# A graph layer on one core: a ring of 24 gathered chunks instead of 84, and all degree rows kept in SBUF

## The chip, the core and the metric

One core of one Trainium2 chip runs the whole kernel. The metric is the device time of one launch in microseconds (us); lower is better. TensorE is called PE here, VectorE DVE, ScalarE ACT, GpSimd POOL and SyncE SP, as the profile does.

## The reference, cut to what matters

There are 50,000 nodes with 128 features each, and 100,000 edges sorted by their target node (each node has at least the edge to itself). For each node the source rows of its edges are summed, and then:

```
h_self  = x @ W_self.T + b_self
messages = x[src] @ W_neigh.T + b_neigh
h_neigh = segment_sum(messages, dst)          # sum over the edges of each target node
out = layernorm(x + relu(h_self + h_neigh))   # over the 128 features
```

The kernel moves the product behind the sum: it sums gathered rows of x per target node and multiplies the sums by W_neigh once. The bias b_neigh then has to be added as often as the node has edges, its degree.

## The kernel before, in words

**The work.** The 50,000 nodes are 391 tiles of 128, taken in 131 groups of three, called trios (`tau` in the code). The self edges are left out of the gather (they go into `wsum` = W_self + W_neigh), so 50,000 edges remain, packed into 391 chunks of 128 edges, three to a trio.

**Preparation (the first 55 us or so).** DVE finds, with help of PE and POOL, where each of the chunks and tiles begins in the edge list. Lists are then made in three parts: chunks 0 to 98 (trios 0 to 32) before the loop, chunks 99 to 197 and 198 to 390 inside the loop by `later_lists(t)` on DVE and PE; the second part is there after loop step 11, the third after step 39. The same code finds the degree of each node (`degrees_start`, `degrees_bits`, `degrees_end`), in three parts too: tiles 0 to 98 before the loop, tiles 99 to 197 by step 19, and the rest by step 55.

**The gather.** POOL issues one indirect DMA for each chunk (line 467): 128 rows of x, 64 KB in all, into slot `c % RING` of the tile `ring`. Before the first chunk of a trio it waits until the trio eight earlier has landed (eight semaphores, `gathered`), and before every chunk from `RING` on until enough trios were summed: `triples_summed >= (c - RING) // 3 + 2`.

**The loop, for each trio.** PE sums gathered rows per target node (`sum_chunks`: two passes for `carry`, line 887, and six matmuls with one-hot tiles `pick`, line 893) and then raises `triples_summed`; DVE builds `pick` beforehand (line 728). ACT copies the sums to `sums_t` (line 994). PE turns the trio's rows of x (line 877), and ACT copies them to `x_t` (line 1002). Then `products` on PE: one bf16 matmul adds the biases, with a tile `degrees_t` of 12 rows as weights (line 908: nine rows hold the degrees of three tiles, three times each since the bias is split in three bf16 parts, and three rows hold 1.0), and twelve fp32 passes follow, six of x at line 912 and six of the sums at line 913; the last raises `h_done`. DVE adds x after the relu (line 739, `y_done`) and takes statistics, ACT normalises (line 1021), and SP stores the result (line 380). PE sums two or three trios ahead of the one whose products it makes. All orders are written out by hand; each engine works through its own list, and semaphores join them.

**SP's queue.** For each trio: load x of that trio (after `y_done` of four trios earlier), load its degree rows from the DRAM scratch `degrees_dram` into one of four tiles `degrees_t` (after `h_done` of four trios earlier), and store the result of the trio six earlier. At loop steps 33 and 66, and once before the loop, `store_degrees` first writes a part of the degrees from SBUF to `degrees_dram` and waits for it to land.

Of the kernel before, what the change touches and what calls it, by code (L numbers as in the profile page):

```python
# [19 lines left out]
BF16 = mybir.dt.bfloat16  # L20
# [5 lines left out]
P = 128  # L26
NODES, DIM, EDGES = 50000, 128, 100000
# [15 lines left out]
COLUMNS = 4  # L43
SPREAD = 99
# [9 lines left out]
TRIO = 3  # L54
TRIOS = -(-TILES // TRIO)
FIRST_TRIOS = SPREAD // TRIO
DEEP = 4
PARTS = 3
BIAS_ROWS = (TRIO + 1) * PARTS
# [14 lines left out]
TIGHT_LOW = 14  # L74
TIGHT_HIGH = 117

RING = 84
GATHER_SEMS = 8
SUM_BANKS = 3
LOAD = 4  # L80
# [91 lines left out]
def build_common_case(nc, ctx, k, x, src, dst, out):  # L172
    def sb(name, shape, dtype=FP32):
        return ctx.enter_context(nc.sbuf_tensor(name, shape, dtype))

    def sem(name):
        return ctx.enter_context(nc.semaphore(name))
# [69 lines left out]
    pick = [sb(f"pick{i}", [P, PICK]) for i in range(DEEP)]  # L247
    sums_t = sb("sums_t", [P, LAP + MARGIN])
    x_t = [sb(f"x_t{i}", [P, TRIO, P]) for i in range(2)]
    degrees_t = [sb(f"degrees_t{i}", [BIAS_ROWS, P], BF16) for i in range(DEEP)]  # L250
    y = [sb(f"y{i}", [P, TRIO, DIM]) for i in range(DEEP)]
    stats = [sb(f"stats{i}", [P, TRIO, 6]) for i in range(DEEP)]
    mean_var = [sb(f"mean_var{i}", [P, TRIO, 2]) for i in range(DEEP)]
# [27 lines left out]
    offsets_known = sem("offsets_known")  # L281
    locals_known = sem("locals_known")
    degrees_done = sem("degrees_done")
    degrees_stored = sem("degrees_stored")
    dve_order = sem("dve_order")
    checks_done = sem("checks_done")
# [2 lines left out]
    gathered = [sem(f"gathered{i}") for i in range(GATHER_SEMS)]  # L289
    sums_cleared = sem("sums_cleared")  # L290
    x_landed = [sem(f"x_landed{i}") for i in range(DEEP)]
    degrees_landed = [sem(f"degrees_landed{i}") for i in range(DEEP)]
    pick_built = sem("pick_built")
    triples_summed = sem("triples_summed")
    sums_placed = sem("sums_placed")
# [4 lines left out]
    h_done = sem("h_done")  # L300
# [9 lines left out]
    def tiles_of(tau):  # L310

        return (1, LAST_ROWS) if tau == TRIOS - 1 else (TRIO, P)
# [17 lines left out]
    with nc.Block() as block_:  # L330

        @block_.sync
        def _(sp):
            sp.dma_start(end_dst[:], dst.rearrange("(b e) -> b e", e=BLOCK)[:, BLOCK - 1:BLOCK].rearrange("b o -> o b"),
                         allow_slow_non_contiguous=True).then_inc(ends_landed, 16)
            for padded, edges in ((dst_padded, dst), (src_padded, src)):
                sp.dma_start(padded[0:EDGES, :].rearrange("(p e) o -> p (e o)", p=EDGE_ROWS),
                             edges.rearrange("(p e) -> p e", p=EDGE_ROWS)).then_inc(padded_stored, 16)
            sp.wait_ge(pads_set, 2)
            for a, padded in enumerate((src_padded, dst_padded)):  # L340
                sp.dma_start(padded[EDGES:EDGES + PAD, :].rearrange("e o -> o e"), pads[:, a, :]).then_inc(padded_stored, 16)
            sp.dma_start(k.ws[:], w_self).then_inc(k.weights_landed, 16)
            sp.dma_start(k.wn[:], w_neigh).then_inc(k.weights_landed, 16)
            sp.dma_start(k.bs_row[:], b_self.rearrange("(a d) -> a d", a=1)).then_inc(k.weights_landed, 16)
            sp.dma_start(k.bn_row[:], b_neigh.rearrange("(a d) -> a d", a=1)).then_inc(k.weights_landed, 16)
            sp.dma_start(k.bn[:], b_neigh.rearrange("(a d) -> a d", a=1).partition_broadcast(P)).then_inc(k.bn_landed, 16)

            def load_x(tau):
                if tau >= DEEP:
                    sp.wait_ge(y_done, tau - DEEP + 1)  # L350
                sp.dma_start(x_in[tau % DEEP][0:tiles_of(tau)[1], 0:tiles_of(tau)[0], :], rows_of(x, tau)).then_inc(x_landed[tau % DEEP], 16)

            def load_degrees(tau):
                tiles, _ = tiles_of(tau)
                if tau >= DEEP:
                    sp.wait_ge(h_done, tau - DEEP + 1)
                sp.dma_start(degrees_t[tau % DEEP][0:tiles * PARTS, :],
                             degrees_dram[tau * TRIO * PARTS:(tau * TRIO + tiles) * PARTS, :]).then_inc(degrees_landed[tau % DEEP], 16)

            def store_degrees(part, j0, j1):  # L360

                sp.wait_ge(degrees_done, part)
                for j in range(j0, j1):
                    sp.dma_start(degrees_dram[j * SPREAD * PARTS:(j + 1) * SPREAD * PARTS, :].rearrange("(p a) n -> p a n", a=PARTS),
                                 degrees[:, j, :].unsqueeze(1).to_broadcast([SPREAD, PARTS, P])).then_inc(degrees_stored, 16)
                sp.wait_ge(degrees_stored, 16 * j1)

            def load_edges():

                sp.dma_start(edge_src[:], src.rearrange("(p e) -> p e", p=EDGE_ROWS)).then_inc(edges_landed, 16)  # L370
                sp.dma_start(edge_dst[:, 0:EDGE_COLS], dst.rearrange("(p e) -> p e", p=EDGE_ROWS)).then_inc(edges_landed, 16)
                sp.wait_ge(next_set, 1)
                sp.dma_start(edge_dst[0:EDGE_ROWS - 1, EDGE_COLS:EDGE_COLS + 1],
                             dst.rearrange("(p e) -> p e", p=EDGE_ROWS)[1:EDGE_ROWS, 0:1],
                             allow_slow_non_contiguous=True).then_inc(next_landed, 16)

            def store(tau):
                tiles, rows = tiles_of(tau)
                sp.wait_ge(result_done, tau + 1)
                sp.dma_start(rows_of(out, tau), result[tau % DEEP][0:rows, 0:tiles, :]).then_inc(stored[tau % DEEP], 16)  # L380

            sp.wait_ge(k.parts_made, 3)
            sp.wait_ge(window_landed[0], 32)
            for q in range(TRIO):
                sp.dma_start(k.bias[q * PARTS:(q + 1) * PARTS, q, :], k.bias_part[:, :, 0, :]).then_inc(k.parts_landed, 16)
                sp.dma_start(k.bias[TRIO * PARTS:BIAS_ROWS, q, :], k.bias_part[:, :, 1, :]).then_inc(k.parts_landed, 16)

            for tau in range(DEEP):
                load_x(tau)
            store_degrees(1, 0, 1)  # L390
            for tau in range(DEEP):
                load_degrees(tau)
            for tau in range(DEEP, TRIOS + DEEP + 2):
                if tau == FIRST_TRIOS:
                    store_degrees(2, 1, 2)
                if tau == FIRST_TRIOS + DEEP:
                    load_edges()
                if tau == 2 * FIRST_TRIOS:
                    store_degrees(3, 2, COLUMNS)
                if tau < TRIOS:  # L400
                    load_x(tau)
                    load_degrees(tau)
                if tau >= DEEP + 2:
                    store(tau - DEEP - 2)
            for i in range(DEEP):
                sp.wait_ge(stored[i], 16 * len(range(i, TRIOS, DEEP)))
# [76 lines left out]
        def _(dve):  # L483
# [6 lines left out]
                dve.wait_ge(dve_order, chain[0])  # L490

            v = nc.vector
            v.memset(pads[:, 0, :], 0).then_inc(pads_set, 1)
            v.memset(pads[:, 1, :], NODES).then_inc(pads_set, 1)
            v.memset(edge_dst[:, EDGE_COLS:EDGE_COLS + 1], NO_NODE).then_inc(next_set, 1)
# [10 lines left out]
            v.memset(k.ones[:], 1.0)  # L506
            v.memset(k.eps[:], EPS)
            v.memset(checks[:], 0.0)
            for i in range(DEEP):
                v.memset(degrees_t[i][:], 1.0)  # L510
            link(v.memset(k.bias[:], 0.0))

            def find_blocks(a, j0, j1):
# [271 lines left out]
            def later_lists(t):  # L785
# [12 lines left out]
                    degrees_bits(1, 2, [t - 11])  # L798
                if t == 13:
                    spread_lists(2, FIRST_TRIOS, 2 * FIRST_TRIOS, FIRST_TRIOS - 1, 2 * FIRST_TRIOS - 1)  # L800
                if t == 19:
                    degrees_end(1, 2)
                if t == 20:
# [14 lines left out]
                    shift_move(2, COLUMNS, (t - 39) // 2)  # L818
                if t == 41:
                    spread_lists(3, 2 * FIRST_TRIOS, ENTRIES // TRIO, 2 * FIRST_TRIOS - 1, TRIOS - 1)  # L820
                if t == 55:
                    degrees_end(2, COLUMNS)
                if t == 60:
# [36 lines left out]
        def _(pe):  # L860
# [36 lines left out]
            def products(tau):  # L897

                b = tau % 2
                tiles, rows = tiles_of(tau)  # L900
                pe.wait_ge(degrees_landed[tau % DEEP], 16 * (tau // DEEP + 1))
                pe.wait_ge(xt_copied, tau + 1)
                if tau >= 2:
                    pe.wait_ge(y_done, tau - 1)
                pe.wait_ge(sums_placed, sums_needed(tau))
                if tau in joined_at:
                    pe.wait_ge(laps_joined, joined_at[tau])
                mm(h_bank[b][0:rows, 0:tiles * DIM], degrees_t[tau % DEEP][:, 0:rows], k.bias[:, 0:tiles, :], start=True, stop=False)  # L908
                for q in range(tiles):
                    h = h_bank[b][0:rows, q * DIM:q * DIM + DIM]  # L910
                    at = (tau * TRIO + q) * P % LAP
                    mm(h, x_t[b][:, q, 0:rows], k.wsum_t[:], start=False, stop=False)  # L912
                    ins = mm(h, sums_t[:, at:at + rows], k.wn_t[:], start=False, stop=(q == tiles - 1))  # L913
                ins.then_inc(h_done, 1)
# [360 lines left out]
```

## Time and profile before

| | us |
|---|---|
| three runs | 804.57, 804.39, 798.32 (median 804.39) |
| the profiled execution, its own time | 803.84 |
| its span, first to last instruction | 802.0 |
| PE busy | 557.8 (70%) |
| DVE busy | 446.4 (56%) |
| POOL busy | 403.5 (50%) |
| ACT busy | 303.2 (38%) |

The rows below come from that one execution. The 1.84 us between its span and its own time lie around the instructions. The granted TensorE clock was 0.865 of full speed on average. Of the DMA engines' time 23.7% went to the queue of SP's transfers and 12.9% to POOL's gathers.

### The profile page before, as it was taken

The page shows a single profiled execution, that of the slowest core. Times are in us where ns is not written, and L with a number is a line of the kernel's source. Part 1 is how long each engine was busy: PE and PEld are TensorE (multiplying, and loading weights), DVE is VectorE, ACT ScalarE, POOL GpSimd, SP SyncE. Part 2 cuts the span into 40 slices and gives each one's busy share as a digit, 9 for nine tenths or more (in the row PEclk, how much of TensorE's full clock was granted, in tenths as well). Part 3 has the DMA queues.
Part 4 walks back from the last instruction along what each step waited for, and adds up shares of the span by engine and source line. Part 5 has one row for each costly group of instructions (what it writes and reads, how often), then busy time and mean ns, then how long its engine had stood idle before and what let it go on. Part 6 is the DMA issues. An engine that isn't in the chain of part 4 may idle for free. (4 is left out here: it accounts for less than half of the span.)

```text
span 802.0 us, 11397 instructions
## 1 busy us (share of the span) xinstructions
PE 557.8 (70%) x3151; PEld 441.7 (55%) x3151; DVE 446.4 (56%) x1927; ACT 303.2 (38%) x789; POOL 403.5 (50%) x424
## 2 busy tenths in 40 slices
PE   2054011069742979888678886978897988999995
PEld 0033001048631767666557675756675776778784
DVE  8880100048812777776566757565554555566765
ACT  0000000025311535444234544535453544566566
POOL 5777777520375656660756666556565666100000
PEclk9998555559955989998879999889997999999998
DMA  2421211123312434453334443444444444433433
GB/s 76 120 56 52 62 52 52 43 60 101 104 52 63 127 113 128 132 150 95 102 93 134 123 133 110 123 114 132 115 136 112 131 123 134 119 105 101 116 104 93
DMA packets 122933, 82.12 MB, mean 102 GB/s; under 512 B 15374, under 2 KB 115894, under 8 KB 122840
## 3 DMA queue, kind: packets, MB, share of 16 engines
q1 hardware_dynamic: 109208, 53.63, 23.7%
q0 software_dynamic: 13664, 27.77, 12.9%
q8 instruction: 26, 0.43, 0.2%
q14 instruction: 35, 0.29, 0.1%
HBM read 55.44 MB, written 26.71 MB: 102 GB/s over the span
## 5 line engine op out<-in xcount | busy, mean ns | idle before, releaser
L467 POOL DMA_INDIRECT ring<-in_x,chunk_src x391 | 378.7, 968 | 271.7 <-issue 110.9
L994 ACT COPY sums_t<-bank 128x496 f32 x131 | 74.8, 571 | 423.9 <-remote 202.2
L893 PE MATMUL bank<-pick,ring 128*128 128x192 f32 (+2 forms) x782 | 231.9, 437 | 4.0 <-DMA ring<-in_x,chunk_src 4.0
L739 DVE SCALAR_TENSOR_TENSOR y<-bank,x_in 128x384 f32<-128x384 f32 x131 | 72.6, 554 | 215.7 <-remote 173.2
L912 PE MATMUL bank<-wsum_t,x_t 128*128 128x128 f32 (+1 forms) x782 | 175.4, 307 | 15.2 <-issue 15.2
L913 PE MATMUL bank<-wn_t,sums_t 128*128 128x128 f32 (+1 forms) x782 | 160.8, 287 | 24.2 <-issue 24.2
L1021 ACT ACTIVATE result<-y,minus_mean,rstd 128x128 f32<-128x128 f32 x391 | 163.4, 486 | 0.0
L893 PEld LDWEIGHTS bank<-pick,ring 128*128 128x128 f32 x782 | 146.1, 210 | 19.0 <-issue 4.3
L912 PEld LDWEIGHTS bank<-wsum_t,x_t 128*128 128x128 f32 (+1 forms) x782 | 126.6, 203 | 40.0 <-issue 39.8
L913 PEld LDWEIGHTS bank<-wn_t,sums_t 128*128 128x128 f32 (+1 forms) x782 | 127.6, 204 | 24.8 <-issue 24.8
L887 PE MATMUL bank<-carry,ring 128*128 128x1 f32 x260 | 44.6, 241 | 106.8 <-DVE pick L728 77.8
L728 DVE TENSOR_SCALAR pick<-columns,local 128x192 f32<-128x192 f32 (+2 forms) x391 | 117.9, 357 | 0.2
L887 PEld LDWEIGHTS bank<-carry,ring 128*128 128x128 f32 x260 | 42.6, 206 | 120.6 <-DVE pick L728 87.5
L759 DVE BATCH_NORM_STATS2 stats<-y 128x6 f32<-128x128 f32 x391 | 87.4, 277 | 0.2
L1002 ACT COPY x_t<-bank 128x384 f32<-128x384 f32 x131 | 63.1, 482 | 54.9 <-remote 24.9
L775 DVE RECIPROCAL rstd<-std 128x3 f32<-128x3 f32 x131 | 21.9, 168 | 105.4 <-ACT std L1011 89.4
L877 PEld LDWEIGHTS bank<-identity,x_in 128*128 128x128 f32 x391 | 54.9, 151 | 41.7 <-issue 12.8
L877 PE MATMUL bank<-identity,x_in 128*128 128x128 f32 x391 | 69.5, 289 | 9.3 <-issue 5.6
L908 PE MATMUL bank<-bias,degrees_t 12*128 12x384 bf16 x131 | 45.6, 348 | 43.2 <-issue 37.1
L908 PEld LDWEIGHTS bank<-bias,degrees_t 12*128 12x128 bf16 x131 | 12.0, 91 | 69.1 <-issue 65.6
L1011 ACT ACTIVATE std<-mean_var,eps 128x3 f32<-128x3 f32 x131 | 40.2, 307 | 0.4 <-DVE mean_var L767 0.4
L767 DVE BATCH_NORM_AGGREGATE mean_var<-stats 128x2 f32<-128x6 f32 x391 | 38.6, 154 | 0.0
(122 smaller groups left out, 207.9 us busy)
## 6 DMA issues: line engine op xcount, KB each, us to landing
x_in<-in_x SPq DMA_DIRECT2D x130, 192.0 KB
out<-result SPq DMA_DIRECT2D x130, 192.0 KB
ring<-in_x,chunk_src POOLq DMA_INDIRECT x391
degrees_t<-degrees_dram SPq DMA_DIRECT2D x130, 2.2 KB
dst_padded<-in_dst SPq DMA_DIRECT2D x1, 390.6 KB
src_padded<-in_src SPq DMA_DIRECT2D x1, 390.6 KB
edge_src<-in_src SPq DMA_DIRECT2D x1, 390.6 KB
edge_dst<-in_dst SPq DMA_DIRECT2D x1, 390.6 KB
```

The source lines that it names most:

```text
L467: nc.gpsimd.indirect_dma_start(ring[:, c % RING, :], None, x, bass.IndirectOffsetOnAxis(ap=chunk_src[:, c:c + 1], axis=0)).then_inc(gather ...
L728: ins = v.tensor_scalar(pick[tau % DEEP][:, PICK_AT[q]:PICK_AT[q] + hi - lo], columns[:, lo:hi], local[:, c:c + 1], None, ALU.is_equal)
L739: v.scalar_tensor_tensor(y[tau % DEEP][0:rows, 0:tiles, :], h_bank[b][0:rows, 0:tiles * DIM].rearrange("p (q d) -> p q d", q=tiles), 0.0, ...
L759: ins = v.bn_stats(stats[b][0:rows, q, :], y[b][0:rows, q, :])
L877: ins = nc.tensor.transpose(xt_bank[b][:, q * P:q * P + rows], x_in[tau % DEEP][0:rows, q, :], k.identity[0:rows, 0:rows])
L887: mm(sums[:, 0:1], ring[:, (tau * TRIO - 1) % RING, :], carry[:, tau - 1:tau], start=True, stop=False, skip_group_check=True)
L893: ins = mm(sums[:, lo:hi], ring[:, c % RING, :], pick[tau % DEEP][:, PICK_AT[q]:PICK_AT[q] + hi - lo], start=(tau == 0 and q == 0), stop=( ...
L912: mm(h, x_t[b][:, q, 0:rows], k.wsum_t[:], start=False, stop=False)
L913: ins = mm(h, sums_t[:, at:at + rows], k.wn_t[:], start=False, stop=(q == tiles - 1))
L994: nc.scalar.copy(sums_t[:, bass.ds(at, SPAN)], sum_bank[tau % SUM_BANKS][:, 0:SPAN]).then_inc(sums_placed, 1)
L1002: nc.scalar.copy(x_t[b][:, 0:tiles, 0:rows], xt_bank[b][:, 0:tiles * P].rearrange("p (q w) -> p q w", q=tiles)[:, :, 0:rows]).then_inc(xt_ ...
L1021: ins = nc.scalar.activation(result[b][0:rows, q, :], y[b][0:rows, q, :], ACT.Identity, bias=minus_mean[b][0:rows, q:q + 1], scale=rstd[b] ...
```

## The change

Two things are changed at once. `RING` goes from 84 to 24. And the four tiles `degrees_t` with one transfer for each trio become one tile with a place for every trio (12 rows, 132 places of 128 bf16 values), filled by four transfers: `store_degrees` issues them itself, one for each of the four groups of 33 trios, behind its wait for the write to DRAM. DVE sets each quarter of the tile to 1.0 beforehand, the first before the loop and the others at steps 12, 40 and 42; SP waits for that (`degrees_set`). PE waits for `degrees_landed` only at trios 0, 33, 66 and 99.

```diff
-RING = 84
+RING = 24
...
-    degrees_t = [sb(f"degrees_t{i}", [BIAS_ROWS, P], BF16) for i in range(DEEP)]
+    degrees_t = sb("degrees_t", [BIAS_ROWS, TRIOS + 1, P], BF16)
...
-            def load_degrees(tau):
-                tiles, _ = tiles_of(tau)
-                if tau >= DEEP:
-                    sp.wait_ge(h_done, tau - DEEP + 1)
-                sp.dma_start(degrees_t[tau % DEEP][0:tiles * PARTS, :],
-                             degrees_dram[tau * TRIO * PARTS:(tau * TRIO + tiles) * PARTS, :]).then_inc(degrees_landed[tau % DEEP], 16)
-
             def store_degrees(part, j0, j1):
 
                 sp.wait_ge(degrees_done, part)
+                sp.wait_ge(degrees_set, j1)
                 for j in range(j0, j1):
                     sp.dma_start(degrees_dram[j * SPREAD * PARTS:(j + 1) * SPREAD * PARTS, :].rearrange("(p a) n -> p a n", a=PARTS),
                                  degrees[:, j, :].unsqueeze(1).to_broadcast([SPREAD, PARTS, P])).then_inc(degrees_stored, 16)
                 sp.wait_ge(degrees_stored, 16 * j1)
+                for j in range(j0, j1):
+                    first = j * FIRST_TRIOS
+                    sp.dma_start(degrees_t[0:TRIO * PARTS, first:first + FIRST_TRIOS, :],
+                                 degrees_dram[j * SPREAD * PARTS:(j + 1) * SPREAD * PARTS, :].rearrange("(t r) n -> r t n", r=TRIO * PARTS)
+                                 ).then_inc(degrees_landed, 16)
...
-            for tau in range(DEEP):
-                load_degrees(tau)
...
-                    load_degrees(tau)
...
+            def set_degrees(j):
+
+                v.memset(degrees_t[:, j * FIRST_TRIOS:(j + 1) * FIRST_TRIOS, :], 1.0).then_inc(degrees_set, 1)
+
...
-            for i in range(DEEP):
-                v.memset(degrees_t[i][:], 1.0)
+            set_degrees(0)
             link(v.memset(k.bias[:], 0.0))
...
+                if t == 12:
+                    set_degrees(1)
...
+                if t in (40, 42):
+                    set_degrees(t // 2 - 18)
...
-                pe.wait_ge(degrees_landed[tau % DEEP], 16 * (tau // DEEP + 1))
+                if tau % FIRST_TRIOS == 0:
+                    pe.wait_ge(degrees_landed, 16 * ((1, 2, COLUMNS, COLUMNS)[tau // FIRST_TRIOS]))
...
-                mm(h_bank[b][0:rows, 0:tiles * DIM], degrees_t[tau % DEEP][:, 0:rows], k.bias[:, 0:tiles, :], start=True, stop=False)
+                mm(h_bank[b][0:rows, 0:tiles * DIM], degrees_t[:, tau, 0:rows], k.bias[:, 0:tiles, :], start=True, stop=False)
```

## Rows read from the trace of the kernel before

**Rows 1.** The page: busy tenths in 40 slices of 20 us.
```profile
PE   2054011069742979888678886978897988999995
...
POOL 5777777520375656660756666556565666100000
```

**Rows 2.** Waits, whole span: engine, line, releaser, us in total, times, longest.
```profile
ACT sums_t L994 <- remote: 202.2, 31, 56.3
...
DVE y L739 <- remote: 173.2, 22, 61.9
...
POOL ring L467 <- DVE chunk_dst L668: 52.8, 3, 32.4
```

**Rows 3.** Timeline of PE, 60 to 170 us: start, us, what.
```profile
63.20 2.90 PE L893 MATMUL bank<-pick,ring 128*128 128x192 f32 x6
...
76.50 0.37 PE L913 MATMUL bank<-wn_t,sums_t 128*128 128x128 f32 x1 [1.03 <-issue]
99.20 0.59 PE L887 MATMUL bank<-carry,ring 128*128 128x1 f32 x2 [22.33 <-issue]
...
165.21 0.59 PE L887 MATMUL bank<-carry,ring 128*128 128x1 f32 x2 [21.15 <-DVE pick L728]
```

**Rows 4.** Timeline of DVE and of ACT, the same stretch.
```profile
97.58 0.56 DVE L739 SCALAR_TENSOR_TENSOR y<-bank,x_in 128x384 f32<-128x384 f32 x1 [39.43 <-remote]
...
119.99 0.57 ACT L994 COPY sums_t<-bank 128x496 f32 x1 [56.30 <-remote]
```

**Rows 5.** Windows: stretch, its us, busy of PE, PEld, DVE, ACT, POOL (with counts), PEclk, DMA share, GB/s.
```profile
66.10:170.50 104.40, 15.83 (x51) 10.77 (x49) 6.08 (x21) 1.80 (x4) 67.66 (x72) 0.55 0.17 49
177.70:210.00 32.30, 31.62 (x194) 25.53 (x193) 28.17 (x124) 18.42 (x48) 0.00 (x1) 0.93 0.33 95
415.00:682.80 267.80, 227.92 (x1348) 181.74 (x1346) 161.72 (x738) 127.03 (x334) 162.55 (x168) 0.94 0.46 125
```

**Rows 6.** Timeline of POOL: the gather behind each pause.
```profile
170.52 0.94 POOL L467 DMA_INDIRECT ring<-in_x,chunk_src  x1 [15.13 <-PE bank L893]
...
257.42 1.05 POOL L467 DMA_INDIRECT ring<-in_x,chunk_src  x1 [6.37 <-remote]
...
407.89 1.04 POOL L467 DMA_INDIRECT ring<-in_x,chunk_src  x1 [4.18 <-remote]
...
470.05 0.94 POOL L467 DMA_INDIRECT ring<-in_x,chunk_src  x1 [0.30 <-issue]
473.13 1.05 POOL L467 DMA_INDIRECT ring<-in_x,chunk_src  x1 [2.14 <-remote]
```

**Rows 7.** Waits of POOL between 415 and 682.8 us.
```profile
POOL ring L467 <- remote: 31.8, 15, 2.8
POOL ring L467 <- PE bank L893: 25.7, 12, 5.5
```

**Rows 8.** Timeline of PE at the end: the sums of the last two trios.
```profile
784.56 1.59 PE L893 MATMUL bank<-pick,ring 128*128 128x192 f32 x6
...
788.26 0.57 PE L893 MATMUL bank<-pick,ring 128*128 128x192 f32 x2
```

**Rows 9.** Groups of instructions, shapes apart: DVE's memsets.
```profile
L747 DVE MEMSET sums_t<- 128x512 f32 x12 | 5.8, 485 | 2.1 <-DVE sums_t L746 1.7 <-issue 0.3
...
L510 DVE MEMSET degrees_t<- 12x128 bf16 x4 | 0.6, 165 | 0.0
```

**Rows 10.** Timeline of DVE, SP and PE around the first degrees.
```profile
8.02 0.74 DVE L515 TENSOR_SCALAR_CACHE_REDUCE below<-bank,limit 99x500 f32<-99x500 f32 x1 [1.08 <-PE bank L864]
...
55.63 0.89 SPq L364 DMA_DIRECT2D degrees_dram<-degrees  x1
58.30 1.41 SPq L357 DMA_DIRECT2D degrees_t<-degrees_dram  x4
...
59.76 0.50 PE L908 MATMUL bank<-bias,degrees_t 12*128 12x384 bf16 x1 [2.78 <-DMA degrees_t<-degrees_dram]
```

**Rows 11.** Waits of SP's DMA queue, whole span.
```profile
SPq L380 <- ACT result L1021: 198.1, 92, 5.3
```

More of the change, by code:

```diff
@@ L283, in build_common_case @@
     degrees_done = sem("degrees_done")
+    degrees_set = sem("degrees_set")
     degrees_stored = sem("degrees_stored")
@@ L291, in build_common_case @@
     x_landed = [sem(f"x_landed{i}") for i in range(DEEP)]
-    degrees_landed = [sem(f"degrees_landed{i}") for i in range(DEEP)]
+    degrees_landed = sem("degrees_landed")
     pick_built = sem("pick_built")
```

## The prediction

> **What bounds the kernel now.** I began with the slices of the page, since a mean hides that this kernel has stretches with different limits [rows 1]. Between 80 and 160 us (fifth to eighth slice) PE is nearly idle while POOL is at 5 to 7 tenths. From 700 us on POOL does nothing and PE stands at 9 tenths. In between both are busy. The waits over the whole span come next [rows 2]: ACT waited 202.2 us ahead of its copy of the sums, DVE 173.2 us ahead of y, with single waits of 56.3 and 61.9 us. For both no releaser is named, though the work they wait for is PE's.
>
> The timelines show what such a wait is. The sums of trio 3 end at 63.20 + 2.90 = 66.1 us [rows 3], but ACT's copy, which waits for them, starts at 119.99 [rows 4]. The first `h_done` is raised by the pass just ahead of 63.20, and DVE's y starts at 97.58. PE has idle gaps of 22.33 and 21.15 us and trickles between them. So PE's finished work is seen by the others 34 to 54 us late. Meanwhile POOL issues one gather after another: 72 in 104.4 us, beside 51 matmuls of PE, while the DMA engines are busy for 0.17 of the time only [rows 5]. This is no lack of bandwidth. In the stretch from 177.7 to 210.0 there is no gather: PE makes 194 matmuls in 32.3 us and is busy for 31.6 of them. That is 6.0 matmuls a microsecond against 0.5.
>
> What ends such a stretch is POOL's own pause [rows 6]: the gather at 170.52 stands behind 15.13 us of idleness, those at 257.42 and 407.89, which end shorter runs of gathers, behind 6.37 and 4.18, and in the steady part the pauses are about 2.14. I read it so: while POOL gathers without a pause, PE's signals are delivered far too slowly, and a pause lets them through. Longer runs need longer pauses. The rows don't show which resource is shared; the argument needs only the pattern.
>
> The steady part, 415 to 682.8 us, then has a simple account. A gather takes 0.94 us and 0.30 to the next [rows 6], 1.25 in all. 168 gathers, 56 trios, fill 168 x 1.25 = 210 us, and the waits of POOL are 31.8 + 25.7 = 57.5 us in 27 pauses of 2.13 [rows 7]: together 267.5 of 267.8. The cadence is 267.8 / 56 = 4.78 us a trio. Without gathers it is 788.26 - 784.56 = 3.70 [rows 8]. The bound is thus this alternation for most trios, PE for the last 26 or so, and for over 100 us at the start neither: the signals are stuck.
>
> **The ring.** With 84 slots POOL may run 26 trios ahead, so at the start it has no reason to pause. With 24 slots chunk c >= 24 waits for `triples_summed` >= (c - 24) // 3 + 2, about six trios ahead. Step by step:
> - Gathers begin at about 38.4 us. Chunks up to 29 need at most three summed trios, known long before. Chunk 30 needs the fourth, whose signal at 66.1 is late. POOL therefore stops after 30 gathers, at 38.4 + 30 x 1.25 = 75.9 us instead of about 155.
> - The signals then get through. The pauses behind shorter and longer runs were 4.18, 6.37 and 15.13 us [rows 6]; 30 gathers are nearest to the run of 33 that ended at 251 us, so I take 6 us. Then DVE makes y and the picks of trio 4, and PE sums trio 4 at about 83.7 us instead of 99.65. From below the pause costs 2.14, from above 15.13.
> - From then on POOL is held by its credits throughout, as it was between 415 and 682.8. I take that cadence, 4.78 us, for trios 4 to 124. Three other things vanish: the stretch up to 170 us, the wait for the list of chunks (52.8 us in all [rows 2]) with the burst behind it, and, on the debit side, the fast trios at 3.70 us, since gathers now accompany nearly all of them. Lists are ready in time: chunk 99 is asked for when trio 26 is summed, and its list is made at step 11.
> - Gathers end about six trios ahead of PE: 6 x 3.70 = 22.2 us, then from the last sum to the end 802.0 - 788.3 = 13.7, as now.
> A ring of six to seven trios can't starve PE at this cadence: it holds some 29 us of work, and a gather needs its own 1.25 us and its landing.
>
> **The degrees.** Four memsets of 128 values (165 ns each) become one of 33 x 128 = 4224. Between 128 and 512 values a memset grows from 165 to 485 ns [rows 9], 0.83 ns a value, so 4224 cost 165 + 4096 x 0.83 = 3.6 us. Behind the old ones DVE idled 1.08 us for PE before 8.02 us [rows 10]; the start becomes later by 3.6 - 0.6 - 1.1 = 1.9 us (none if the fill runs several values at a time, 2.9 if the idle time can't be used). The three inside the loop, 3.6 us each, stand on DVE ahead of the next y and picks; with DVE busy 161.72 of 267.8 us [rows 5], 0.4 of each lies in slack. I count 1 us each, 3 in all, between 0 and 11.
>
> At the start the tile's transfer follows the write to DRAM. Now the write is issued at 55.63, the loads at 58.30, and PE goes on at 59.76. One load of all 297 pieces is as large as the write, which needed 2.67 us: 1.2 us later for PE, at most 4 if it takes twice as long. This hardly shows in POOL's pause, which is set by the gathers.
>
> What is removed: 131 issues on SP at 1.41 / 4 = 0.35 us each. SP waited 198.1 us for ACT's results alone [rows 11], so this lies in idle time, and I take nothing for it. PE has one wait less for each trio; where gathers hold up its signals that might bring a little, where they don't its matmuls are the limit. I take 0, and as the other bound 0.05 us x 131 = 6.6 us. At trios 33, 66 and 99 PE needs a load that SP issued three or more trios earlier, over 10 us: hidden. If that cover were gone, it would cost about 3 us each.
>
> **The sum.** Trio 4 summed from 83.7 + 1.9 = 85.6. 120 trios x 4.78 = 573.6: 659.2. Six trios and the tail, 35.9: 695.1. Memsets 3: 698. Around the span lie 803.84 - 802.0 = 1.8: 700 us. The profiled execution is within 0.6 us of the median 804.39, so I compare with that directly: 0.87 of it.
>
> **The rivals.**
> - *Small steps with a pause for each (slower).* In the steady part POOL made 168 / 27 = 6.2 gathers between pauses. The handshake could settle at three, each with the pause of 2.13 us: 3.75 + 2.13 = 5.88 us a trio, and the sum is 85.6 + 706 + 35.9 + 3 + 1.8 = 832. It decides from a cadence of 5.65. For it: a short ring gives credits one trio at a time. Against: the old ring did so too once it was full.
> - *POOL becomes the only bound (faster).* If evenly spread gathers leave PE's signals alone, the cadence is POOL's own 3.75: 85.6 + 450 + 35.9 + 3 + 1.8 = 576. For it: the 3.70 without gathers. Against: the steady part, where POOL was held back likewise and lost 1.03 us for each trio.
> - *The first stretch stays.* If the stuck signals are released by something other than POOL's pause, PE reaches trio 6 at 176 us as now, and 118 trios at 4.78 follow: 176 + 564 + 35.9 + 3 + 1.8 = 781.
> - *The gathers are innocent.* [Rows 5] show 0.5 matmuls a microsecond beside gathers and 6.0 without. Then both would have a third cause, the ring would change nothing, and only the memsets would be left: 804 + 1.9 + 3, near 808. The Trainium skill's page "SBUF — State Buffer", section "Who interferes with whom", speaks for this rival: only the port pair that VectorE and GpSimd share causes contention, and a DMA never contends with a compute engine, so gathers could not hold up TensorE. The rows here disagree with a reading of that rule that extends it to signals: PE stands still beside gathers while DVE is idle too.
>
> **How the numbers follow.** Forecast 0.78, small steps 0.06, POOL the bound 0.07, the first stretch stays 0.05, gathers innocent 0.04. Within the forecast the cadence matters most: with a pause only after nine gathers it is 3.75 + 2.13 / 3 = 4.46, 38 us less; after 4.5 gathers it is 5.17, 47 us more. The start adds 9 us and the memsets and the first load up to 11 upwards, the start 4 and PE's lighter list 7 downwards; not all at once. The range is 655 to 745. A difference under 1% can't be told from none. Faster by over 1%: 0.78 + 0.07 + 0.05 = 0.90; same 0.04; slower 0.06.
>
> **What the changed profile would show.** Slices of PE from the fifth on at 6 tenths or more; POOL busy to near the end in every slice at about 6 to 7 tenths, with no wait for `chunk_dst`; gathers 415 to 682.8 still about 168; no single wait of ACT or DVE over 15 us; POOL's first long pause near 76 to 78 us; three memsets near 3.6 us in the loop, and four issues of `degrees_t`. I am wrong if the cadence beside gathers differs from 4.78, if POOL's first pause is as long as 15 us, or if PE waits for `ring`.

## The result and the profile after

The changed kernel took 707.26 us (median of 4 runs, 706.41 to 711.72), the kernel before beside it 804.48 (4 runs, 798.32 to 807.9): a ratio of 0.881, with a 95% interval of 0.8745 to 0.8875. The profiled execution took 706.77 us with a span of 705.0; its granted clock averaged 0.928 against 0.865. The prediction said 700 in a range of 655 to 745.

One thing has to be said beside this number. In the runs of this study the unchanged kernel before showed two times: about 800 us in four sets of runs (this one among them) and about 582 us in two others. All that follows about a gain holds where the kernel before takes 800 us. Where it took 582, neither the ring of 24 nor the wait alone changed the time, and the changed kernel as it is was not run.

The slices of the page after, to be read against [rows 1]: 40 slices, now of 17.6 us.
```profile
PE   2036388988797878697987879788898978979995
...
POOL 3777565666666656555655646565555666555600
```
The hole of four slices in PE is one slice deep (the fifth, at 3), and POOL gathers to near the end. Waits over the whole span, to be read against [rows 2]: engine, line, releaser, us in total, times, longest. "Remote" stands where the view names no releaser.
```profile
ACT sums_t L1000 <- remote: 192.5, 43, 24.4
...
POOL ring L464 <- remote: 85.2, 39, 4.8
...
DVE y L740 <- remote: 78.1, 28, 10.4
...
POOL ring L464 <- PE bank L898: 54.8, 30, 5.8
```
The longest wait of ACT fell from 56.3 to 24.4 us and that of DVE from 61.9 to 10.4; POOL's waits are now many and short. The wait of POOL for `chunk_dst` is gone. Now the start. The timelines of PE, of SP's queue (the first load of the degrees) and of POOL between 61 and 90 us, to be read against [rows 3] and [rows 6]:
```profile
64.36 0.49 PE L914 MATMUL bank<-bias,degrees_t 12*128 12x384 bf16 x1 [4.45 <-DMA degrees_t<-degrees_dram]
...
72.76 1.59 PE L898 MATMUL bank<-pick,ring 128*128 128x192 f32 x6
...
85.86 0.50 PE L914 MATMUL bank<-bias,degrees_t 12*128 12x384 bf16 x1 [7.74 <-ACT x_t L1008]
...
89.29 2.35 PE L898 MATMUL bank<-pick,ring 128*128 128x192 f32 x6
```
```profile
61.26 0.32 SPq L364 DMA_DIRECT2D degrees_t<-degrees_dram  x1
```
```profile
79.75 0.94 POOL L464 DMA_INDIRECT ring<-in_x,chunk_src  x1 [0.30 <-issue]
85.51 0.94 POOL L464 DMA_INDIRECT ring<-in_x,chunk_src  x1 [4.81 <-remote]
```
POOL stopped at 79.75 + 0.94 = 80.7 us and waited 4.81 us. PE stands still for the 7.74 us before 85.86, 2.6 of them before POOL's stop, and goes on 0.35 us after POOL does. The trio summed at 72.76 is trio 4, before POOL's stop; trio 5 follows 16.5 us later.

Windows of after: stretch, its us, busy of PE, PEld, DVE, ACT, POOL (with counts), PEclk, DMA share, GB/s, to be read against [rows 5].
```profile
80.00:160.00 80.00, 63.18 (x361) 50.60 (x361) 58.39 (x228) 33.97 (x86) 47.50 (x49) 0.89 0.40 108
89.30:415.00 325.70, 273.11 (x1565) 215.89 (x1565) 245.42 (x969) 148.08 (x387) 197.28 (x198) 0.92 0.46 123
100.00:640.00 540.00, 457.26 (x2647) 361.89 (x2648) 356.39 (x1522) 252.84 (x662) 326.81 (x334) 0.93 0.46 124
415.00:640.00 225.00, 192.34 (x1130) 152.59 (x1130) 117.04 (x573) 108.35 (x286) 136.25 (x142) 0.94 0.46 124
```
Between 80 and 160 us PE now makes 361 matmuls, 4.5 a microsecond, where it made 51 in the 104.4 us of [rows 5]. From 100 to 640 us POOL makes 334 gathers, 111.3 trios: 4.85 us a trio. The steady stretch of before had 4.78. So the whole kernel now runs at about the rate that its steady part had. Of the 97.0 us between the two spans, 76.4 are gained up to the sums of trio 5, which start at 89.3 instead of 165.7, and 20.7 between trio 5 and trio 124 (579.7 us instead of 600.4): less time lost up to 415 us, fewer fast trios at the end. The sums of trio 124 start at 669.0, 36.0 us ahead of the end, as before (35.9).

### The profile page after: what moved, and what is told of

Same layout as the page of the kernel before. It is cut to its first block and busy times, and to the rows that moved or that the text cites. A ratio compares the mean times of both kernels' runs of the same rounds, so it can differ in the third digit from the quotient of the medians.

```text
span 705.0 us, 11177 instructions
## 1 busy us (share of the span) xinstructions
PE 551.2 (78%) x3151; PEld 434.3 (62%) x3151; DVE 461.1 (65%) x1927; ACT 303.2 (43%) x789; POOL 410.1 (58%) x424
## 5 line engine op out<-in xcount | busy, mean ns | idle before, releaser
L464 POOL DMA_INDIRECT ring<-in_x,chunk_src x391 | 385.2, 985 | 244.9 <-issue 104.4
L918 PE MATMUL bank<-wsum_t,x_t 128*128 128x128 f32 (+1 forms) x782 | 170.9, 302 | 1.9 <-issue 1.9
L919 PE MATMUL bank<-wn_t,sums_t 128*128 128x128 f32 (+1 forms) x782 | 156.5, 282 | 2.0 <-issue 1.8
L898 PEld LDWEIGHTS bank<-pick,ring 128*128 128x128 f32 x782 | 144.4, 208 | 20.7 <-issue 5.2
L918 PEld LDWEIGHTS bank<-wsum_t,x_t 128*128 128x128 f32 (+1 forms) x782 | 123.4, 198 | 27.6 <-issue 27.5
L919 PEld LDWEIGHTS bank<-wn_t,sums_t 128*128 128x128 f32 (+1 forms) x782 | 124.1, 200 | 1.5 <-issue 1.5
L729 DVE TENSOR_SCALAR pick<-columns,local 128x192 f32<-128x192 f32 (+2 forms) x391 | 119.8, 361 | 0.2
L892 PEld LDWEIGHTS bank<-carry,ring 128*128 128x128 f32 x260 | 41.2, 199 | 87.2 <-DVE pick L729 78.5
L882 PE MATMUL bank<-identity,x_in 128*128 128x128 f32 x391 | 71.1, 294 | 7.4 <-DMA x_in<-in_x 4.4
```

The source lines that it names most:

```text
L464: nc.gpsimd.indirect_dma_start(ring[:, c % RING, :], None, x, bass.IndirectOffsetOnAxis(ap=chunk_src[:, c:c + 1], axis=0)).then_inc(gather ...
L729: ins = v.tensor_scalar(pick[tau % DEEP][:, PICK_AT[q]:PICK_AT[q] + hi - lo], columns[:, lo:hi], local[:, c:c + 1], None, ALU.is_equal)
L882: ins = nc.tensor.transpose(xt_bank[b][:, q * P:q * P + rows], x_in[tau % DEEP][0:rows, q, :], k.identity[0:rows, 0:rows])
L892: mm(sums[:, 0:1], ring[:, (tau * TRIO - 1) % RING, :], carry[:, tau - 1:tau], start=True, stop=False, skip_group_check=True)
L898: ins = mm(sums[:, lo:hi], ring[:, c % RING, :], pick[tau % DEEP][:, PICK_AT[q]:PICK_AT[q] + hi - lo], start=(tau == 0 and q == 0), stop=( ...
```

## The experiments

Three explanations stood at first. A: POOL's wait for summed trios, which comes after 24 chunks and makes it pause, is the whole gain. B: fewer slots matter by themselves (where the gathers land). C: the degree part brings something, by shorter lists on SP and PE or by its issues.

**The ring alone, and the wait alone.** The first is the kernel before with `RING` at 24. The second keeps 84 slots and changes the wait only:
```
+AHEAD = 24
...
-                if c >= RING:
-                    pool.wait_ge(triples_summed, (c - RING) // TRIO + 2)
+                if c >= AHEAD:
+                    pool.wait_ge(triples_summed, (c - AHEAD) // TRIO + 2)
```


> The kernel before with RING = 24 and nothing else. Theory A (POOL's unpaused gathers hold up PE's signals; the ring acts through POOL's earlier wait): nearly the whole gain is here, and a little more, since the 3.6 us memset at the start, the three in the loop and the longer first load of degrees are absent: 700 us, between 690 and 712. Rival C (the 131 small transfers were the burden, on SP's queue or on PE's waits): little is gained, 780 to 805.

> The kernel before with its tile of 84 slots, but POOL waits for triples_summed as with 24 slots. Theory A: the same as with RING = 24 alone, within 5 us, first pause of POOL after 30 gathers. Rival B (the size of the tile, the spread of the writes in SBUF or the reuse of slots matters): near 804.

Measured: 581.97 us (ratio 1.0002, 0.9974 to 1.0030) and 582.13 us (0.9994, 0.9976 to 1.0011), and the kernel before itself took 582.43 us in this set (19 runs, 578.58 to 583.96). No theory had this, and the set can't decide between A, B and C, since there was nothing to gain. The profile of the ring alone shows what is different. A window of the same stretch as the first of [rows 5], and the slices of the page:
```profile
66.10:170.50 104.40, 101.24 (x648) 83.06 (x647) 98.05 (x402) 60.40 (x155) 79.61 (x82) 1.00 0.54 148
```
```profile
PE   2017899999999889999997989999999999999994
...
POOL 4777777777777777777777767777777777777300
```
POOL made 82 gathers in this stretch, more than the 72 of [rows 5], and PE was busy for 101.24 of 104.4 us. POOL issued 231 gathers in one run, from 38.2 to 337.0 us, and where ACT waited for the sums, its copy began at most 0.9 us behind them. So a long run of gathers is not enough to hold up PE's signals: a condition outside the kernel must be present too. With it absent the cadence is 3.98 us a trio, near the 3.70 of [rows 8], and ring and wait are worth nothing.

The two levels differ only where gathers run. Up to the first gather there is no difference (38.4 us in before, 38.2 here), and the last six trios, from the sums of trio 124 to those of trio 130, take 22.2 us in both (766.06 to 788.26 and 543.69 to 565.89). So the 800 us are not those of a chip on which everything is slower.

**A shorter ring yet.** After with `RING = 12`, same set.

> The changed kernel with RING = 12. Theory A: two trios are summed early, so POOL pauses after 18 gathers, before PE's signals are stuck; the start gains some 10 us, and the cadence stays near 4.9 us a trio: 697 us. The rival of a too short ring: POOL may gather for a trio only when the one three earlier is summed, PE waits for ring, and the cadence grows to 5.9 us or more: 800 us or more.

Measured: 601.14 us, 1.0317 of before (1.0280 to 1.0353). Here too there was no lag to undo. POOL's waits with a named releaser end with PE's sums:
```profile
POOL ring L464 <- PE bank L898: 43.2, 29, 6.3
```
The cadence is 4.09 us against 3.98. It says nothing on the stuck signals. That a lead of two trios is on the short side is likely, but not shown alone: how much of the 19 us is the degree part's wasn't measured at this level.

**Gathers spaced out.** After, with a memset of 128x256 behind each gather. POOL works through its list in order, so the next gather stands behind the memset; each memset also waits for the one before it:
```
+                if c:
+                    pool.wait_ge(spaced_out, c)
+                nc.gpsimd.memset(spacer[:], 0.0).then_inc(spaced_out, 1)
```


> The changed kernel with a POOL memset of 128x256 behind each gather, which spaces the gathers from 1.25 to about 1.6 us. If what counts is how much POOL sends per unit of time (each gather needs a little more of a shared path than the 1.25 us in which it is issued), then PE's signals are no longer late and POOL's pauses vanish: 4.8 us a trio from three gathers at 1.6, the total about as the changed kernel, 690 to 710. If only POOL's full stops let signals through, the memsets add to the cadence: 3 x 0.35 = 1.05 us for each trio, 125 us in all, 830.

Measured in the first set: 640.78 us, 1.1001 of before (1.0963 to 1.1038). With 1.47 us from gather to gather POOL needs 4.41 us a trio and becomes the bound: the cadence was 4.40, and in the repeat below PE waited 35.7 us for the ring.

**Both kernels again.** The next set looked whether the 582 us would come back.

> The changed kernel once more, beside the kernel before on the same chip. Two readings of the first four experiments, in which the kernel before took 582 us and not 804: theory D, the late signals belong to the chip (or to its surroundings at the time) and not to the kernel; then on a chip without them this is the kernel before plus the memsets and the longer first load, 582 + 1 to 8 us, and on a chip with them 707 against 804. Rival E: something of the ring and degree parts together differs from the parts alone; then the ratio of 0.88 comes back even where the kernel before takes 582 us.

> The kernel before, for its profile. On a chip without late signals POOL gathers 84 and more chunks in one run, and yet ACT's copy of the sums starts 0.1 us behind them, PE is at 9 tenths from about 60 us on. On a chip with them the profile is that of 802 us again, with waits of 56 and 62 us near the start.

The 582 us did not come back: before had a median of 800.33 (7 runs), after 707.06 (700.6 to 710.17), ratio 0.882 (0.8751 to 0.8890), which repeats the first result. Rival E is therefore not tested here; the wait alone answers it further below. The profile of before again has a run of 93 gathers from 38.3 to 155.9 us, single waits of 57.0 (ACT) and 62.2 us (DVE), and PE at zero in the fifth and the eighth slice:
```profile
PE   2054021049733988889498887988888888999995
```

**Four kernels for the cause of the lag.** The next set was to tell whether POOL's issuing, the number of pieces or the bytes hold up the signals. `sp_loads` is before with 24 slots and no gathers at all: SP loads the 192 KB of each trio from neighbouring rows, so that other rows are summed. `narrow` is before with gathers of 128 B an index, and the other three quarters of each slot left at zero:
```
-                nc.gpsimd.indirect_dma_start(ring[:, c % RING, :], None, x,
+                nc.gpsimd.indirect_dma_start(ring[:, c % RING, 0:DIM // 4], None, x.rearrange("n (a d) -> (n a) d", a=4),
```


> Again the kernel before with 84 slots, POOL waiting as with 24, in the hope of a chip with late signals. If the kernel before takes about 800 here: theory A gives 700 (690 to 712), with the first pause of POOL after 30 gathers; rival B (size of the tile, reuse of slots) 800; rival C (the degree transfers) 785 to 800. If it takes about 582, this one does too.

> The changed kernel with a POOL memset of 128x256 behind each gather; gathers 1.47 us apart, and 640 us on a chip without late signals. On a chip with them: if a gather keeps a shared path busy for a little more than the 1.25 us in which POOL issues it, the spacing lets the signals through without pauses, the lags shrink to a microsecond or two, and the time comes down from 707 towards 640 to 660. If only POOL's full stops let signals through, the cadence is 4.4 + 1.1 us or more and the time 750 to 790.

> The kernel before with RING = 24 and no gathers: SP loads the ring, 192 KB for each trio in one plain transfer of neighbouring rows of x, so the sums are of other rows than the reference's. The same bytes land in the same tile. If the bytes or their landing hold up PE's signals, the cadence on a chip with late signals stays near 4.8 us a trio and the time near 700. If it is POOL's issuing, the lags are gone: PE at 3.70 us a trio, 575 to 590, and the same on any chip.

> The kernel before (84 slots) with gathers of 128 bytes for each index instead of 512, from x seen as rows of 32 values; three quarters of each slot stay at zero and the sums are not the reference's. The number of pieces, of gathers and of completions is unchanged. If the bytes matter, the first stretch loosens and the time falls to between 580 and 650; if the issuing or the pieces matter, it stays at 800 with PE idle between 80 and 160 us (on a chip without late signals it says nothing: 582).

Before took 582.2 us in this set (13 runs), and again nothing lagged: the wait alone 582.36 us (1.0012, 0.9987 to 1.0038), spaced 642.33 (one run), SP's loads 576.01 (one run), narrow 585.58 (one run, with its zeroing of the ring on POOL at the start). So these can't tell the causes apart. One thing they do suggest: with no gather at all the kernel took 576.01 us in its one run, 6 less than the median of before, so where signals are delivered at once the gathers cost about 1%.

**The wait alone where before takes 800 us.** The same kernel as the wait alone, once more.

> The kernel before with 84 slots and POOL waiting as with 24, a third time. Where the kernel before takes about 800: theory A gives 700 (690 to 712), POOL's first pause after 30 gathers, and with it the whole gain without the degree part and without fewer slots; rivals B and C give 785 to 800. Where the kernel before takes about 582, this one does too and the question stays open.

Now before had 801.47 us (6 runs), and the wait alone took 701.40 (4 runs, 693.47 to 705.64): ratio 0.8706, 0.8616 to 0.8795. The whole gain is there with all 84 slots and with the degrees as they were. B and C fall, A stands, and E with its ring and degree parts together is not needed. Its timeline of POOL at the first stop, and its window:
```profile
75.57 0.94 POOL L468 DMA_INDIRECT ring<-in_x,chunk_src  x1 [0.30 <-issue]
82.33 0.94 POOL L468 DMA_INDIRECT ring<-in_x,chunk_src  x1 [5.82 <-remote]
```
```profile
100.00:640.00 540.00, 457.46 (x2689) 364.03 (x2690) 350.97 (x1533) 256.52 (x672) 326.02 (x336) 0.94 0.46 126
```
It stops at 76.5 us for 5.82 us, as the prediction had it (75.9 and 6), and makes 336 gathers in the 540 us in which after made 334.

**Spaced where before takes 800 us.** The same kernel as in "Gathers spaced out".

> The changed kernel with a POOL memset of 128x256 behind each gather, once more; its gathers are 1.47 us apart at least, and it takes 641 us where the kernel before takes 582. Where the kernel before takes about 800: if each gather keeps a shared path busy for a little more than the 1.25 us in which POOL issues it, the spacing lets PE's signals through without full stops: lags of 1 to 2 us, POOL's waits few, 640 to 670. If only full stops let signals through, three gathers take 4.4 us and 1.1 us or more of stops come on top for each trio: 750 to 790.

Before 801.39 us (7 runs), spaced 705.97 (702.97 to 710.41), ratio 0.8793 (0.8738 to 0.8849). The same time as after without spacers, though each gather is now followed by POOL's own work. A piece of POOL's timeline, then the window, then waits:
```profile
301.85 0.95 POOL L467 DMA_INDIRECT ring<-in_x,chunk_src  x1 [0.17 <-issue]
302.80 0.33 POOL L472 MEMSET spacer<- 128x256 f32 x1
303.29 0.95 POOL L467 DMA_INDIRECT ring<-in_x,chunk_src  x1 [0.16 <-issue]
```
```profile
100.00:640.00 540.00, 457.46 (x2657) 366.18 (x2657) 374.07 (x1517) 255.26 (x661) 443.55 (x666) 0.92 0.46 124
```
```profile
ACT sums_t L1006 <- remote: 136.8, 40, 8.2
...
POOL ring L467 <- PE bank L904: 30.0, 22, 3.8
POOL ring L467 <- remote: 20.0, 17, 1.4
```
The longest wait of ACT without a named releaser is 8.2 us, against 24.4 in after; where it waits for the sums, its copy starts at most 6.7 us behind them, against 14.2 in after. POOL made its first 42 gathers without a pause, where after stopped for 4.81 us behind 30. POOL's waits come to 50.0 us in 39, against 140.0 us in 69 in after. The spacers filled much of what had been pauses, and the cadence hardly changed: 4.96 and 4.87 us a trio. Neither expectation holds. Long pauses are thus not needed for the signals to get through; the numbers fit a picture in which time off gathers counts for each trio, whether one stop or three spacers give it, but no run tests that picture by itself. In this condition 3 x 1.47 = 4.41 us a trio was still too fast, and POOL had to wait on top of it.

## Why the prediction was right

**The mechanism.** "While POOL gathers without a pause, PE's signals are delivered far too slowly" was read from [rows 3 to 6]; the wait alone shows that bounding how far POOL runs ahead, with its first stop after 30 gathers, is the whole gain. Two additions are needed. The lag exists only in a condition that the profile of before can't show to be one, since its pattern looks like a property of the kernel. And it seems to be the density of gathers that matters, rather than the absence of a pause (argued from the spaced kernel, not shown). The rival that the gathers are innocent, with 808 us, falls where before takes 800: moving only POOL's wait changed the time by 13%. Where before takes 582 it would have been right, and the same prediction would have missed by the whole gain: that the result was taken at 800 us was luck, which the 0.78 did not allow for. The Trainium skill's page "SBUF — State Buffer", section "Who interferes with whom", by which a DMA never contends with a compute engine, gives no account of the 800 us; the 582 us agree with it (648 matmuls of PE beside 82 gathers in 104.4 us). What the two share while the lag is there is not shown.

**What the prediction overlooked in the trace of before.** It is not only that the others see PE's signals late. PE's own passes are held up too, in the middle of `products`, where PE's list has no wait. Three rows of PE's timeline between those of [rows 3], and one of DVE's:
```profile
68.79 0.27 PE L912 MATMUL bank<-wsum_t,x_t 128*128 128x128 f32 x1 [1.02 <-issue]
...
71.59 0.27 PE L912 MATMUL bank<-wsum_t,x_t 128*128 128x128 f32 x1 [2.53 <-issue]
...
75.09 0.37 PE L913 MATMUL bank<-wn_t,sums_t 128*128 128x128 f32 x1 [3.23 <-issue]
```
```profile
98.05 1.10 DVE L728 TENSOR_SCALAR pick<-columns,local 128x192 f32<-128x192 f32 x3
```
Idle time of this kind ahead of the passes of lines 912 and 913 comes to 15.2 + 24.2 = 39.4 us in before, to 1.9 + 1.8 in after and to 0.0 in the ring alone at 582 us. Signals to PE aren't late in the same stretch: DVE's picks end at 98.05 + 1.10 = 99.15 us and PE starts on them at 99.20 [rows 3], with POOL gathering all the while. So what is held up beside the gathers is what PE sends and, in part, PE's own progress. A supply of instructions that runs short would explain the held passes, but not that ACT sees at 119.99 us sums that had ended at 66.1; no run tests it.

**Term by term**, in the profiled execution of after, the start of trio 124's sums being predicted for 662.2 us and found at 669.0:
- *The start.* Predicted: trio 4 summed at 85.6. Found: 72.8, that is 12.8 earlier. The step that failed is the one that let trio 4 wait for the end of POOL's stop: its picks and PE's signals got through while POOL was still gathering, and it was trio 5 that hung (89.3). That varies from run to run: in the profiled repeat of after trio 4 is summed at 86.3 and in the wait alone at 83.5, where the prediction had it (85.6, and 83.7 without the memset), with trio 5 at 92.6 and 88.9. POOL stopped at 80.7 us and not at 75.9 + 1.9 = 77.8. The long memset at the start cost 2.8 us and not 1.9 (first gather at 41.2, not 38.4), near the upper end of 0 to 2.9: DVE starts it at 7.03 after 0.83 us of idle time, so the idle time that was to cover it was spent ahead of it. The first 30 gathers took 39.5 us and not 37.5. The pause was 4.81, not 6.
- *The cadence, 4.78 for 120 trios.* Found: (669.0 - 72.8) / 120 = 4.97, which is 22.6 us more. The gap from trio 4 to 5 alone is 16.5 us, 11.7 more than the cadence; the rest is 119 trios at 4.87 instead of 4.78, 10.9 us. The 11.7 only undo the early trio 4; the 10.9 are the real error of the sum, and the 3 us that it had for the memsets in the loop lie in them. The step that was mis-sized is taking the cadence of 415 to 682.8 us for the whole way. From trio 71 on, which starts at 416.8, it is 4.76 us, as predicted; from trio 5 to 71 it is 4.96. In that first part DVE also makes the later lists: it is busy 245.42 of 325.7 us there and 117.04 of 225 behind it. With SP's loads, at 582 us and without a gather, the same two parts have 4.01 and 3.81 us, the same 0.2 apart, so this part of the cadence is not the gathers'.
- *The memsets of the degrees.* 3.6 us each were predicted and 3.578 measured. Lines, shapes apart, of after:
```profile
L493 DVE MEMSET degrees_t<- 12x4224 bf16 x4 | 14.3, 3578 | 3.6 <-issue 3.6
```
- *The first load.* Predicted: 1.2 us later, at most 4. It is issued at 61.26 and PE goes on at 64.36 [timelines of after, above]: 3.1 us from issue to use, where [rows 10] have 1.46. That is 1.6 us. PE's wait there grew from 2.78 to 4.45.
- *The removed issues on SP and waits on PE.* Taken as worth nothing; the 0.05 us a wait of the other bound stands in no row. After and its repeat, 707.26 and 707.06 us, stand 5.8 us above the wait alone at 701.40. The sum had 1.9 + 3 = 4.9 for the degree part. But the three ran in different sets, the intervals of the ratios (0.8745 to 0.8875 and 0.8616 to 0.8795) overlap, and after also has 24 slots where the wait alone has 84. So neither the size nor the degree part as the cause of the 5.8 us is shown; what is seen is its 2.8 us ahead of the first gather, and no gain.
- *The tail.* 35.9 predicted, 36.0 found.
- *The signs.* Three of those named did not come: the fifth slice of PE stands at 3 and not at 6 or more, one wait of ACT is 24.4 us and not under 15, and POOL's first long pause begins at 80.7 us and not near 76 to 78. They belong to the start, where trio 5 hung.

**The rivals.** Small steps with a pause for each (832 us): the handshake stayed at between five and six gathers for each wait of POOL (391 gathers, 69 waits), not three. POOL as the only bound (576 us): this did not happen at the 800 us level, where even spaced gathers were held back. At the other level the kernel with the ring alone took 582 us, close to that number, but with PE as its bound, for before took it too. The first stretch stays (781 us): gone, by the slices above.

The lowest median where before takes 800 us is that of the wait alone, with 701.40 us: the bound on POOL's lead that the ring of 24 brings, without the fewer slots and without the degree part. Where before takes 582 us it is level with before, so it costs nothing there.

**What stays open.** What sets the level: it was constant within each set and different between sets, and chip number 9 showed both (number 15 was seen at 582 us only, number 7 at 800 only; that of the first set is not known). So it is not the chip alone. What PE and the gathers share when it is high: is it POOL's issuing, the number of pieces, or their bytes? `sp_loads` and `narrow` were made for that but only met the 582 us. The ring alone was not run at the 800 us level; the wait alone stands for it.

## What to carry to other kernels

When waits with no named releaser are tens of microseconds long while the engine that should release them has finished, plot them against what another engine issues without a stop, and bound how far that engine may run ahead by a wait; this costs one number and was worth 12 to 13% where before took 800 us, and nothing where it took 582. Don't put a second change beside it: the degree part brought no gain that can be seen, and what it costs can't be told from the rest. And before trusting either, run the unchanged kernel in more than one set, for a gain can belong to the condition of the chip that the first profile met.

## What the runs showed of the hardware

- One and the same program took 582 or 800 us, 1.37 times as long, with agreement within 1 to 2% inside each set. The granted clock differed with it, 0.979 in the ring alone and 0.865 in before, but it followed PE's idle time here and did not make it: in the first window of [rows 5] PE has 0.15 of its time busy at a clock of 0.55, and at its start the passes at 68.79 and 71.59 us, already behind gaps of 1.02 and 2.53 us, still take 0.27 us, and only those from 75.09 us on take 0.37.
- In the 800 us condition POOL's pause grew with the run of gathers, 1.25 us apart, that it ended: 4.8 to 5.8 us behind 30, 6.37 behind 33, 15.13 behind 93. With gathers 1.47 us apart the first pause, behind 42, was 1.17 us.
- In that condition, while gathers ran, PE's passes inside `products` started in steps of about 0.7 us or multiples of it: 68.79, 71.59, 75.09 and 76.50 us in before. What sets this step is not shown.
- In that condition a trio beside gathers took 4.8 to 5.0 us in four kernels (before's steady part, after, the wait alone, spaced), whether POOL spaced its gathers or burst and stopped. Without gathers it took 3.70. All four have three gathers a trio, so no run tells a cost of each gather from a cost of each trio, nor on what.
